# Router logits by a stationary, padded router in four column quarters, and turned back

## The reference, cut to what matters

```python
x = x + attention(layernorm(x), ctx, ctx)       # 128 sequences of 64 tokens, 128 wide, causal
xt = layernorm(x).reshape(-1, 128)              # 8192 tokens
logits = xt @ gate_w.T                          # 8192 x 8
_, idx = jax.lax.top_k(logits + beta, 2)
probs = jax.nn.sigmoid(take_along_axis(logits, idx))
out = x + sum_of_two_experts(xt, idx, probs) + shared_expert(xt)   # each: (silu(g) * u) @ down, 128 -> 256 -> 128
```

## Time and profile before

| | us |
|---|---|
| median of 3 runs | 423.53 |
| lowest, highest | 419.73, 426.79 |
| profiled execution | 422.82 |
| its span, first to last instruction | 421.1 |
| mean granted TensorE clock | 0.977 |

### The profile page before, as it was taken

The page is one execution under the profiler, slowest core; times in us unless marked ns, Lnnn a source line. Parts: engine busy times, 40 slices in busy tenths (PEclk is TensorE's granted clock), DMA queues, the critical chain, the costliest instruction groups (busy, mean ns, idle before and its releaser), DMA issues.

```text
span 421.1 us, 10737 instructions
## 1 busy us (share of the span) xinstructions
PE 394.0 (94%) x3056; PEld 350.1 (83%) x3056; DVE 300.8 (71%) x1324; ACT 254.3 (60%) x554; POOL 267.0 (63%) x312
## 2 busy tenths in 40 slices
PE   7668999999999999989999999999999999999970
PEld 3556787778778887669999999989999999999970
DVE  3498799998999988776986666556667666666650
ACT  2568899999999994346566556553122565665520
POOL 7658788888888866617887888875200045555551
PEclk9699999999999999999999999999999999999995
DMA  8943344677444121244555666673332123432221
GB/s 241 342 126 102 102 126 127 214 239 229 126 131 156 59 60 58 73 116 98 92 82 81 91 82 91 90 111 55 50 78 55 35 26 47 53 39 26 22 25 12
DMA packets 61480, 41.76 MB, mean 99 GB/s; under 512 B 5688, under 2 KB 56384, under 8 KB 61424
## 3 DMA queue, kind: packets, MB, share of 16 engines
q1 hardware_dynamic: 49296, 30.69, 26.4%
q0 software_dynamic: 12128, 10.40, 17.4%
HBM read 24.17 MB, written 16.90 MB: 98 GB/s over the span
## 4 chain that ended last, share of the span: by engine, by line
PE 81%; POOL 4%; issue 4%; DVE 4%; DMA 3%; ACT 1%; SPq 1%; POOLq 0%; DVEq 0%; ACTq 0%
PE gu_pair L1275 30%; PE bank L1299 15%; PE bank L1202 7%; PE bank L1214 6%; PE bank L1193 6%; PE gu_pair L1144 3%; PE gu_pair L1125 3%; PE gu_pair L1163 3%; PE bank L1241 2%; PE gu_pair L1154 2%; DMA tile_in<-sorted_rows 1%; PE gu_pair L1113 1%; PE gu_pair L1133 1%; PE gu_pair L1180 1%; POOL rstd L417 1%
## 5 line engine op out<-in xcount | busy, mean ns | idle before, releaser
L509 POOL DMA_INDIRECT out<-t_out,tile_in x64 | 100.1, 1564 | 88.2 <-DVE t_out L1047 76.8
L1275 PE MATMUL gu_pair<-tile_T,W_slot 128*128 128x128 f32 x1024 | 124.8, 275 | 0.0
L1275 PEld LDWEIGHTS gu_pair<-tile_T,W_slot 128*128 128x128 f32 x1024 | 119.5, 192 | 0.1
L683 ACT ACTIVATE t_silu<-gu_pair 128x512 f32<-128x512 f32 (+1 forms) x78 | 46.4, 594 | 104.3 <-PE gu_pair L1275 96.2
L1007 DVE TENSOR_TENSOR t_hid<-t_silu,gu_pair 128x512 f32<-128x512 f32 (+1 forms) x78 | 53.0, 680 | 48.3 <-PE gu_pair L1275 47.9
L1299 PE MATMUL bank<-W_down,t_hid 128*128 (+1 forms) x620 | 82.7, 276 | 0.2 <-DVE t_hid L1007 0.2
L458 POOL DMA_INDIRECT sorted_rows<-rows,slot x64 | 63.6, 994 | 23.4 <-issue 16.8
L673 ACT ACTIVATE W_slot<-W 128x512 f32 x128 | 73.0, 621 | 6.1 <-issue 4.6
L1299 PEld LDWEIGHTS bank<-W_down,t_hid 128*128 128x128 f32 x620 | 75.4, 192 | 1.0 <-issue 0.8
L469 POOL DMA_INDIRECT left_in<-sorted_rows,left_index x27 | 26.5, 981 | 16.1 <-DVE left_index L926 8.2
L417 POOL TENSOR_TENSOR rstd<-var_eps,minus_half 128x4 f32<-128x4 f32 x32 | 33.0, 1032 | 5.7 <-DVE var_eps L738 5.3
(11 more groups left out here) (153 smaller groups left out, 637.0 us busy)
## 6 DMA issues: line engine op xcount, KB each, us to landing
tile_in<-sorted_rows SPq DMA_DIRECT2D x91, 66.5 KB, 2.0
x_sb<-x SPq DMA_DIRECT2D x16, 256.0 KB, 4.6
c_T<-ctx_cols SPq DMA_DIRECT2D x16, 256.0 KB, 2.9
c_sb<-ctx SPq DMA_DIRECT2D x16, 256.0 KB, 3.4
out<-acc SPq DMA_DIRECT2D x16, 256.0 KB, 3.4
sorted_rows<-padding SPq DMA_DIRECT2D x1, 2128.0 KB, 9.4
sorted_rows<-left_in SPq DMA_DIRECT2D x27, 66.5 KB, 2.1
sorted_rows<-rows,slot POOLq DMA_INDIRECT x64, 3.6
```

The lines of the kernel that those rows point to most:

```text
L509: e.indirect_dma_start(out_flat, bass.IndirectOffsetOnAxis(ap=tile_in[:, tiles_of(i)[0] % NR, ID:ID + 1].bitcast(I32), axis=0), t_out[:, q ...
L683: e.activation(t_silu[:, 0:n * M], gate_up_pair[i % 2][0][:, 0:n * M], ACT.Silu).then_inc(s_t_silu, 1)
L1275: r = e.matmul(bank[:, c:c + P], w, tile_T[:, i % TX, tile], start=True, stop=True, skip_group_check=True)
```

## The change

`router_T` is padded with zeros from 8 to 32 columns. `route` makes it the stationary operand and lets the tokens move; each of the four tiles of tokens writes its own 32 partitions of `L_turned`, so that each uses another quarter of the array's columns. The result has the logits on the partitions and the tokens along the row. DVE copies these 128 x 128 values to SBUF (`copy_logits_T`, at the very beginning of its pass `it = g+4`, ahead of `variances(it, 0)`), and PE transposes them (`turn_logits`, in its pass `it = g+3`, behind `transpose_xn(it)` and ahead of `shared_down_mm(it-5)`). After it, L has the tokens on the partitions again, eight logits of every 32 columns. DVE also clears the padding once, at `it = 1`.

```diff
+        L_turned = O[:, 2 * P:3 * P]
+        L = O[:, 3 * P:4 * P].rearrange("p (t e) -> p t e", t=GT)[:, :, 0:E]
...
+            def copy_logits_T(g):
+                e.wait_ge(s_logits_turned, g + 1)
+                if g:
+                    e.wait_ge(s_logits, g)
+                e.tensor_copy(logits_T[:], L_turned).then_inc(s_logits_T, 1)
...
             for it in range(G + 6):
+                if 4 <= it < G + 4:
+                    copy_logits_T(it - 4)
                 if it < G:
                     variances(it, 0)
...
-                e.tensor_copy(router_T[:], X[:, 0:E]).then_inc(s_router_T, 1)
+                    e.memset(router_T[:, E:LE], 0.0)
+                    e.tensor_copy(router_T[:, 0:E], X[:, 0:E]).then_inc(s_router_T, 1)
...
-                    r = e.matmul(L[:, i * E:(i + 1) * E], xn2_T[:, g % RT, i * P:(i + 1) * P], router_T[:],
+                    r = e.matmul(L_turned[i * LE:(i + 1) * LE], router_T[:], xn2_T[:, g % RT, i * P:(i + 1) * P],
                                  start=True, stop=True, skip_group_check=True)
-                r.then_inc(s_logits, 1)
+                r.then_inc(s_logits_turned, 1)
+
+            def turn_logits(g):
+                e.wait_ge(s_logits_T, g + 1)
+                e.transpose(O[:, 3 * P:4 * P], logits_T[:], ident[:]).then_inc(s_logits, 1)
...
                 if it < G:
                     transpose_xn(it)
+                if 3 <= it < G + 3:
+                    turn_logits(it - 3)
```

More of the change, by code:

```diff
@@ L59, in build @@
     WN = 2 * M
+    LE = P // GT
     FILL = 4
@@ L107, in build @@
         router = sb("router", [E, D])
-        router_T = sb("router_T", [D, E])
+        router_T = sb("router_T", [D, LE])
         RX, RC, RR, RG, RT = 5, 4, 7, 4, 4
@@ L134, in build @@
         code = sb("code", [P, GT])
+        logits_T = sb("logits_T", [P, P])
         tanh_l = sb("tanh_l", [P, GT, E])
@@ L196, in build @@
         A, C, O, X, G0, U0, G1, Y = banks
-        L = O[:, 0:GT * E]
+        L_turned = O[:, 2 * P:3 * P]
+        L = O[:, 3 * P:4 * P].rearrange("p (t e) -> p t e", t=GT)[:, :, 0:E]
         R = O[:, P:P + GT * Q]
@@ L266, in build @@
         s_xn2_transposed, s_xn2_T = sem("xn2_transposed"), sem("xn2_T")
+        s_logits_turned, s_logits_T = sem("logits_turned"), sem("logits_T")
         s_logits, s_biased, s_tanh, s_sigmoid = sem("logits"), sem("biased"), sem("tanh"), sem("sigmoid")
@@ L640, in tanh_logits @@
                     e.wait_ge(s_sigmoid, g)
-                e.activation(tanh_l[:, :, :], L.rearrange("p (t e) -> p t e", t=GT), ACT.Tanh, scale=0.5).then_inc(s_tanh, 1)
+                e.activation(tanh_l[:, :, :], L, ACT.Tanh, scale=0.5).then_inc(s_tanh, 1)
             def silu_gates(g):
@@ L777, in bias_logits @@
                     e.wait_ge(s_top_index, g)
-                e.tensor_tensor(biased[:, :, :], L.rearrange("p (t e) -> p t e", t=GT),
+                e.tensor_tensor(biased[:, :, :], L,
                                 beta_all[:, :].rearrange("p (a e) -> p a e", a=1).broadcast_to([P, GT, E]),
```

## The result

| | before | changed |
|---|---|---|
| median of 20 runs, us | 422.15 | 425.75 |
| lowest to highest | 419.73 to 426.79 | 424.19 to 426.95 |
| profiled execution, span | 421.1 | 425.2 |

The changed kernel is slower by 0.87% (ratio 1.0087, 95% interval 1.0070 to 1.0105), 3.6 us between the medians. The forecast was 428.8, within 2%, with a range of 423.5 to 435.0: right in direction and in calling the change smaller than 2%, too high by 3 us.

A forecast was written before the change was run, and what follows sets the result against it. PE was taken to bound the kernel, with DVE and ACT close behind. Steady loop 3.1 us plus ends 0.8, 0.8, 1.0 and 0.3 gave + 6.0 on the profiled 422.82: 428.8 us, range 423.5 to 435.

The forecast's parts named there:

- The loop: Steady passes: attend, DVE's residual, variances and copy, then PE's waiting transpose; 0.28 us a pass, 3.1 us over 11 passes.
- the cover: PE's wait for DVE's copy before the transpose hides the route's length, up to r = 0.89 us.
- The distance r: PE, from the start of route to the next step: taken as 0.5 us, bounds 0.22, 0.89 and 1.22.
- The ends: Start and last three passes, where the copy isn't hidden: + 0.8, + 0.8, + 1.0 and + 0.3 us.
- the clock: Rival, chance 0.06: PE waits longer at the start, one more slow-clock stretch costs 1.7 us: 430.5 or more.
- The drained quarters: Rival, chance 0.20: route's quarters neither overlap nor switch freely, r = 1.22, a pass costs 0.61 us more: 433.8.
- The cheaper hand-over: Rival, chance 0.20: copy takes 0.15, next step follows the transpose after 0.11, a pass costs 0.06 us: 425.0.
- The gain that comes through: Rival, chance 0.03: quarters overlap fully and DVE's copy isn't late, 0.48 us gained in each of 16 passes: 415.6.
- ACT's 0.70 of waiting: ACT waits 0.70 us a pass for DVE's shift; claimed to take the later shift caused by the copy.

The follow-up runs named there:

- copy_late: Changed kernel with DVE's copy moved behind variances(it, 0), no work added: 449.4 to 450.1 us in three of four executions, 442.5 in one.
- the repeated routes: Changed kernel with route's four matmuls issued twice, three or five times over: 426.02, 426.84 and 431.98 us.
- old_route_turned: Kernel before, old route kept, with DVE's copy and PE's transpose added, the turned values not used: 428.16 us, ratio 1.0141.
- filled pair: Kernel before and changed kernel, both with thirty-two dummy matmuls in PE's waits of the first five passes: 418.28 and 423.09 us.
- quarters_five: Changed kernel with route's four matmuls issued five times over: 431.98 us.
- quarters_alone: The change without copy and transpose, bias and tanh reading the turned result as it stands, so wrong experts are chosen: 420.44 us, ratio 0.9946 to before.
- turn_in_down: Changed kernel with turn_logits moved behind the first of the four tiles of shared_down_mm: 423.43 us, ratio 1.0040 to before.

## Why the prediction was right, and what in it was off

**The loop.** Right, and the whole of the steady loss. The transpose starts 2.95 us behind `attend`'s end (forecast 2.94), the pass is 10.10 (forecast 10.13), DVE's wait for `attend` persists. `copy_late` shows that 1.40 us more in the loop is 1.40 us more in the pass, the repeated routes that PE's own time counts only once it is past the cover, and `old_route_turned` that such a pass needs no quarters. Two sizes in it were off. The step behind the transpose follows after 0.16 us instead of 0.20, so a pass costs 0.256 us and not 0.28, 0.3 us over 11 passes, and more at the ends. And the cover ends at a route of 0.79 us, not 0.89: the prediction kept the route's start at 106.94 and put nothing for the way into the quarters, which takes 0.09. At r = 0.37 this changed nothing.

**The distance r.** Taken as 0.5, measured 0.37: full overlap of the quarters (0.21 for eight records) and 0.16 once, where I had assumed pairs overlapping by half. As argued, it changed nothing in the steady pass; it took 0.13 off the 18th pass and off the start.

**The ends.** Start and last passes were forecast at 0.81 + 0.76 + 0.99 + 0.34. With the clock out of play the way to the first `shared_down_mm` is + 1.02, against 0.81 + 0.28 = 1.09 by the forecast; the last three passes grew by 0.69, 0.89 and 0.12 in the plain pair and by 1.65 together in the filled one, against 0.76, 0.99 and 0.34. The sum of 6.0 is 4.8 in the filled pair. (Of the 3 us by which the forecast was too high, 0.7 is its base: it was added to the profiled execution's 422.82, and the median of 20 runs is 422.15.)

**The term that was missing** is the rest, 1.2 us: 4.8 in the filled pair, 3.6 in the plain one. I had put the clock down as a rival that could only add to the loss. In fact the filling is worth 3.9 us to the kernel before and 2.7 to the changed one: before has more to lose at half clock. The profiles agree: with the filling the first `shared_down_mm` starts 3.72 us earlier in the kernel before (49.24 to 45.52) and 2.54 us in the changed one (49.08 to 46.54). Between the two plain profiles the difference that counts is the second dip near 41 us, which before has and the changed kernel hasn't: from the second route to the third before takes 11.22 us, and 9.61 with the filling (34.52 to 44.13), the changed kernel 9.75, and 9.76 with it (35.50 to 45.26). Why the one falls there and the other doesn't stays open. PE waits for ACT's silu just before, 1.26 us in the kernel before and 1.01 in the changed one, but `old_route_turned` waits 1.01 us too and falls. The first step behind this wait, in the kernel before:

```profile
39.46 1.25 PE L1202 MATMUL bank<-xn_T,shared_gu 128*128 128x512 f32 x2 [1.26 <-ACT silu_g L650]
```

in the changed kernel, where it takes the shortest time:

```profile
40.66 1.12 PE L1220 MATMUL bank<-xn_T,shared_gu 128*128 128x512 f32 x2 [1.01 <-ACT silu_g L655]
```

and in `old_route_turned`, at half clock:

```profile
40.91 1.77 PE L1216 MATMUL bank<-xn_T,shared_gu 128*128 128x512 f32 x2 [1.01 <-ACT silu_g L652]
```

How often each kernel falls there over many executions isn't settled either, as only profiled ones show it. And the 4.8 us lies only just outside the interval of the plain difference, 3.0 to 4.4 us.

**The rivals.** The drained quarters were priced by r = 1.22; measured r is 0.37, so quarters one after another with two drains are refuted. `quarters_five`, which has just the length of 1.22, has a pass of 10.53 where the rival had 9.845 + 0.61 = 10.46 (the 0.09 in front of the route are missing in it): what a route of that length costs was right, only it takes five routes to reach it. The cheaper hand-over, with a copy of 0.15 us and the next step 0.11 behind the transpose, didn't come: they are 0.29 and 0.16. The gain that comes through didn't come either: the changed kernel is slower, and `quarters_alone` shows no gain in the steady loop even without copy and transpose. The prediction said that without any wait PE would gain 0.20 us a pass and that ACT's 0.70 of waiting takes the later shift. In `turn_in_down` neither holds: without the wait the pass is 9.95, the chain runs over ACT, and ACT's idle time per pass was not that loop's slack. It didn't matter for the number, because the DVE loop was the longer one.

## What to carry to other kernels

A step that is shortened on the busiest engine by sending its result through another engine gains only what is left after the round trip: before counting the saving, find what the other engine has to do first, and whether that in turn waits for the engine that is to be helped. Where several engines are each busy for over 90% of the pass, look for loops that cross them (over two passes too), and price the change by the longest loop, not by the share of busy time; idle time on an engine isn't the slack of a loop through it. In the start-up phase of this kernel, with waits of one or two microseconds on TensorE, dummy matmuls into a bank not yet used took off 3.9 us, about as much as the change had added (3.6).

## What the runs showed of the hardware

- Four float32 matmuls of 128 moving columns into the four column quarters overlap fully: eight more records cost 0.21 us, the first eight 0.37. The way into the quarters costs another 0.09 us in front of them.
- A weight load of 32 columns has a record of 106 ns and eight of them follow within 0.16 us; of 128 float32 columns, in `shared_down_mm`, it has 191 ns.
- With a wait of 1.67 us in every pass (1.87 in one) the granted clock fell from 2.4 to 1.2 GHz in four of nine passes, and then 16 records took 3.04 to 3.51 us instead of 1.96; with a wait of 0.27 us in the steady passes of the changed kernel it stayed at 2.4 GHz.
- Near 40 us the same wait of 1.01 us was followed by a fall in `old_route_turned` and by none in the changed kernel.
